# A graph attention layer: source maxima and shift spreads moved ahead of the last value tiles, two value tiles moved into the first steps

## The reference

```
for h in range(8):
    Wx = x @ Ws[h] + Wb[h]
    s = Wx[v_tgt] @ a_w[h, :d] + Wx[v_src] @ a_w[h, d:] + a_b[h]
    s = leaky_relu(s, 0.2)
    alpha = segment_softmax(s, v_tgt, n)     # minus the segment's maximum, exp, divided by the sum
    out[h] = segment_sum(alpha[:, None] * Wx[v_src], v_tgt, num_segments=n)
x = layernorm(x + stack(out, axis=1))
```

## Time and profile before

| | us |
|---|---|
| median of 3 runs | 2437.59 |
| lowest and highest | 2435.18, 2441.69 |
| the profiled execution's own time | 2438.18 |
| its span | 2436.4 |

### The profile page before, as it was taken

How to read it: one execution, slowest core, us unless ns; L and a number is a source line. 1 busy time by engine, 2 the same in 40 slices (tenths; PEclk the granted TensorE clock), 3 DMA queues, 4 the chain that set the end, 5 groups by cost and what they waited for, 6 DMA issues and landing times. The chain is left out here.

```text
span 2436.4 us, 38708 instructions
## 1 busy us (share of the span) xinstructions
PE 2099.4 (86%) x14446; PEld 1586.3 (65%) x14446; DVE 1608.4 (66%) x3166; ACT 1020.9 (42%) x1498; POOL 644.7 (26%) x472
## 2 busy tenths in 40 slices
PE   6888978998899998899998899998885996888784
PEld 5885537887777887677887777887672553333331
DVE  8995264778564877564778554877535045899964
ACT  1112225667344666344666344666320032144442
POOL 0000025100553100554100554100520000386763
PEclk9999989999999999999999999999997997998886
DMA  1011311889321889321889320879327000000001
GB/s 58 34 44 45 103 46 51 146 146 165 78 66 40 147 142 158 87 66 33 147 143 164 87 66 26 151 140 161 96 110 186 12 4 21 1 0 0 1 0 42
DMA packets 488150, 195.74 MB, mean 80 GB/s; under 512 B 441077, under 2 KB 457461, under 8 KB 487969
## 3 DMA queue, kind: packets, MB, share of 16 engines
q1 hardware_dynamic: 487969, 193.31, 38.0%
HBM read 62.94 MB, written 25.45 MB: 36 GB/s over the span
## 5 line engine op out<-in xcount | busy, mean ns | idle before, releaser
L667 PE MATMUL psum<-turned_probability_parts,values_high 125*128 125x125 bf16 x1600 | 281.5, 222 | 59.3 <-DVEq L1520 23.7
L856 DVE CUSTOM_DVE_ANT_0 probabilities<-psum,counts 125x1250 f32<-125x1250 f32 x160 | 233.5, 1459 | 130.0 <-PE psum L669 129.7
L1367 ACT ACTIVATE probabilities<-probabilities,row_peaks 125x1250 f32<-125x1250 f32 x160 | 214.5, 1341 | 181.2 <-DVE row_peaks L860 181.0
L669 PE MATMUL psum<-turned_probability_parts,values_low 125*128 125x125 bf16 x1600 | 280.8, 221 | 0.0
L668 PE MATMUL psum<-turned_probability_parts,values_high 125*128 125x125 bf16 x1600 | 280.5, 221 | 0.0
L1529 DVE SCALAR_TENSOR_TENSOR probability_parts<-probabilities,row_masses,probability_parts 125x1250 bf16<-125x1250 f32 x160 | 245.7, 1536 | 9.2 <-ACT probability_parts L1377 8.6
L1890 POOL TENSOR_TENSOR logs_and_shifts<-logs_by_source,target_shifts_spread 125x1250 f32<-125x1250 f32 x80 | 208.0, 2616 | 127.0 <-ACT target_shifts_spread L2023 67.9
L1377 ACT ACTIVATE probability_parts<-probabilities,row_masses 125x1250 bf16<-125x1250 f32 x160 | 214.0, 1338 | 40.3 <-DVE row_masses L868 34.0
L2129 PE MATMUL psum<-probabilities_turned,values_and_ones 125*65 125x512 f32 (+1 forms) x480 | 198.6, 560 | 21.8 <-ACT probabilities_turned L2040 11.4
L667 PEld LDWEIGHTS psum<-turned_probability_parts,values_high 125*128 125x128 bf16 x1600 | 159.0, 99 | 80.7 <-issue 79.0
L450 ACT ACTIVATE norm_std<-norm_moments,norm_eps 125x1 f32<-125x1 f32 x120 | 35.2, 294 | 365.8 <-DVE norm_moments L446 365.8
(11 more groups left out here) (292 smaller groups left out, 5123.0 us busy)
## 6 DMA issues: line engine op xcount, KB each, us to landing
weight_stage<-in_L_gnn_m_w SPq DMA_DIRECT2D x32, 256.0 KB, 2.7
block_inputs_kept<-nodes SPq DMA_DIRECT2D x8, 896.0 KB
counts_kept<-counts_by_target_rows SPq DMA_DIRECT2D x10, 625.0 KB, 3.5
counts_by_target<-counts_kept SPq DMA_DIRECT2D x1, 6103.5 KB
logs_kept<-counts SPq DMA_DIRECT2D x1, 5468.8 KB
nodes<-block_inputs_kept SPq DMA_DIRECT2D x12, 448.0 KB
turned_probability_parts<-probability_parts SPq DMA_TRANSPOSE x320, 3.6
logs_by_source<-logs_kept SPq DMA_DIRECT2D x1, 4375.0 KB
```

The costliest lines, as they stand in the source:

```text
L667: pe.matmul(out, lh, rh, start=first, stop=False, skip_group_check=True)
L669: return pe.matmul(out, ll, rh, start=False, stop=last, skip_group_check=True)
L856: dve.tensor_tensor_reduce(prob[0:TILE, T % 2, :], scores, fx.count_src[0:TILE, i, 0:NODES], scale, MASKED, ALU.add, ALU.max, p[:, 0:1]).t ...
L1367: nc.scalar.activation(prob[0:TILE, T % 2, :], prob[0:TILE, T % 2, :], ACT.Exp, bias=fx.peak[0:TILE, T % 2, 1:2], accum_out=fx.mass[0:TILE ...
```

## The change

The arithmetic is the same. The order and three places in memory change:

- All of head 0's peaks, its `shift_of`, its turning and its three spread pieces come ahead of value tiles 6 to 9 on TensorE. VectorE does ten peaks, then two value tiles, and so on, in place of six (or four) peaks and one.
- Value tiles 8 and 9 (`EARLY_VALUES` = 8) are made within steps 0 and 1, in bank 7: on TensorE behind the step's source spread and ahead of `weigh(0)`, on VectorE behind the peaks of steps 0 and 1.
- On TensorE the source spreads of cuts 1 and 2 of head 0 stand behind value tiles 2 and 4.
- Each probability and shift buffer is a tensor of its own (rounded up to 32 bytes). Shift buffer 0 and probability buffers 0 and 1 lie behind `nodes_turned`, shift buffer 1 and probability buffers 2 and 3 on it. ScalarE's wait for all value tiles is gone; TensorE waits for the first eight before `weigh(0)`, and for the tenth before it turns head 1's shift.

The diff, without the lines in which only an index changes form:

```diff
@@ -1826,8 +1826,12 @@
         x_t = packer(nc, TURNED_AT)("nodes_turned", [128, CHUNKS, NODES], F32)
-        prob = packer(nc, TURNED_AT)("probabilities_turned", [128, 4, NODES], F32)
-        shifts = packer(nc, TURNED_AT + PLANE)("target_shifts_spread", [128, 2, NODES], F32)
+        place = packer(nc, TURNED_AT + PLANE)
+        shifts = [place("target_shifts_spread_0", [128, NODES], F32)]
+        prob = [place(f"probabilities_turned_{k}", [128, NODES], F32) for k in range(2)]
+        place = packer(nc, TURNED_AT)
+        shifts.append(place("target_shifts_spread_1", [128, NODES], F32))
+        prob += [place(f"probabilities_turned_{k}", [128, NODES], F32) for k in range(2, 4)]
         offset = packer(nc, SLOT_A_AT + TILES * NODES * 4 + 16)("logs_and_shifts", [128, 2, NODES], F32)
@@ -1853,10 +1857,15 @@
+        def value_bank(t):
+
+            return t % 2 if t < EARLY_VALUES else 7
+
         def region(n):
...
         PIECES = ((0, 500), (500, 1000), (1000, NODES))
+        EARLY_VALUES = TILES - 2
         PEAKS = 3 * TILES
@@ -1962,16 +1971,25 @@
             dve.wait_ge(cols_ready, 3)
-            for t in range(TILES):
-                if t < HALF:
-                    for n in range(6 * t, 6 * t + 6):
-                        peaks(0, n)
-                    if t == HALF - 1:
-                        shift_of(0)
-                else:
-                    for n in range(4 * (t - HALF), 4 * (t - HALF) + 4):
-                        peaks(1, n)
+            for n in range(TILES):
+                peaks(0, n)
+            value(0)
+            value(1)
+            for n in range(TILES, 2 * TILES):
+                peaks(0, n)
+            value(2)
+            value(3)
+            for n in range(2 * TILES, PEAKS):
+                peaks(0, n)
+            shift_of(0)
+            value(4)
+            value(5)
+            for n in range(TILES):
+                peaks(1, n)
+            for t in range(6, EARLY_VALUES):
                 value(t)
+            for n in range(TILES, 2 * TILES):
+                peaks(1, n)
@@ -1990,6 +2008,8 @@
                         peaks(g, n)
+                if T < TILES - EARLY_VALUES:
+                    value(EARLY_VALUES + T)
             for k in range(2):
@@ -2033,11 +2053,10 @@
-            act.wait_ge(v_ready, TILES)
             for T in range(STEPS):
...
                 act.wait_ge(scored, T + 1)
-                nc.scalar.activation(prob[0:TILE, T % 4, :], prob[0:TILE, T % 4, :], ACT.Exp,
+                nc.scalar.activation(prob[T % 4][0:TILE, :], prob[T % 4][0:TILE, :], ACT.Exp,
                                      bias=column[0:TILE, j, HEADS3 + h:HEADS3 + h + 1], scale=1.0 / UNIT3).then_inc(exped, 1)
@@ -2068,10 +2087,14 @@
             def value(t):
-                if t >= 2:
+                if t == EARLY_VALUES:
+                    pe.wait_ge(piece_copied, 4)
+                elif t > EARLY_VALUES:
+                    pe.wait_ge(v_ready, t)
+                elif t >= 2:
                     pe.wait_ge(v_ready, t - 1)
                 for c in range(CHUNKS):
-                    mm = pe.matmul(bank(t % 2)[0:TILE], x_t[:, c, cols(t)], lw.w_sb[:, c, :], start=(c == 0),
+                    mm = pe.matmul(bank(value_bank(t))[0:TILE], x_t[:, c, cols(t)], lw.w_sb[:, c, :], start=(c == 0),
                                    stop=(c == CHUNKS - 1))
@@ -2094,7 +2117,7 @@
                 elif h == 1:
-                    pe.wait_ge(piece_copied, 4)
+                    pe.wait_ge(v_ready, TILES)
                 else:
@@ -2139,16 +2162,20 @@
             pe.wait_ge(bias_ready, 1)
-            for t in range(1, TILES):
-                if t in (2, 4, 5, 8):
-                    n = (2, 4, 5, 8).index(t) + 1
-                    spread_sources(n // 3, n % 3)
+            value(1)
+            value(2)
+            spread_sources(0, 1)
+            value(3)
+            value(4)
+            spread_sources(0, 2)
+            value(5)
+            spread_sources(1, 0)
+            shift_turned(0)
+            for k in range(3):
+                shift_piece(0, k)
+            for t in range(6, EARLY_VALUES):
                 value(t)
-                if t == 6:
-                    shift_turned(0)
-                if t in (7, 8, 9):
-                    shift_piece(0, t - 7)
-            pe.wait_ge(v_ready, TILES)
+            spread_sources(1, 1)
             pe.wait_ge(ones_set, 1)
@@ -2162,6 +2189,10 @@
                         shift_piece(h + 1, j - 5)
+                if T < TILES - EARLY_VALUES:
+                    value(EARLY_VALUES + T)
+                if T == 1:
+                    pe.wait_ge(v_ready, EARLY_VALUES)
                 if T >= 1:
```

More of the change, by code:

```diff
@@ L1889, in _ @@
                     pool.wait_ge(scored, T - 1)
-                nc.gpsimd.tensor_tensor(offset[0:TILE, T % 2, :], lw.logs[0:TILE, j, :], shifts[0:TILE, h % 2, :],
+                nc.gpsimd.tensor_tensor(offset[0:TILE, T % 2, :], lw.logs[0:TILE, j, :], shifts[h % 2][0:TILE, :],
                                         ALU.add).then_inc(offset_ready, 1)
@@ L1982, in _ @@
                     dve.wait_ge(pv, T - 3)
-                dve.scalar_tensor_tensor(prob[0:TILE, T % 4, :], region(3)[0:TILE], bend[0:TILE, j, h:h + 1],
+                dve.scalar_tensor_tensor(prob[T % 4][0:TILE, :], region(3)[0:TILE], bend[0:TILE, j, h:h + 1],
                                          offset[0:TILE, T % 2, :], ALU.max, ALU.add).then_inc(scored, 1)
@@ L2022, in shift_piece @@
                 act.wait_ge(piece, 4 * h + 2 + k)
-                nc.scalar.activation(shifts[0:TILE, h % 2, a:z], bank(7)[0:TILE, 0:z - a], ACT.Copy).then_inc(piece_copied, 1)
+                nc.scalar.activation(shifts[h % 2][0:TILE, a:z], bank(7)[0:TILE, 0:z - a], ACT.Copy).then_inc(piece_copied, 1)
             def copy_out(h):
@@ L2128, in weigh @@
                 for a, z in CUTS:
-                    mm = pe.matmul(region(0)[0:WIDTH, a:z], values[0:TILE, j, h, :], prob[0:TILE, T % 4, a:z],
+                    mm = pe.matmul(region(0)[0:WIDTH, a:z], values[0:TILE, j, h, :], prob[T % 4][0:TILE, a:z],
                                    start=(j == 0), stop=(j == TILES - 1))
```

2 lines of the change are left out of this document (1 added, 1 removed).

## The result

The changed kernel took 2452.34 us (median of 6 runs, 2446.76 to 2455.55) against 2440.30 (6 runs of the kernel before beside it, 2435.18 to 2441.96). The ratio is 1.0049, with a 95% interval of 1.0032 to 1.0066: 12.0 us slower, where 9 was forecast and the range reached to 2454. Measured once more, 12 runs against 29 of the kernel before, it gave 1.0029 (1.0014 to 1.0044), 7 us. The two together say slower by 0.3 to 0.5%, some 7 to 12 us.

A forecast was written before the change was run, and what follows sets the result against it. The chain through GpSimd's first sums to step 4's score, then mostly VectorE and TensorE, was taken as the bound. Step 4 7.7 later plus 1.3 for shift buffer 1 gave 9.0 on 2438.18: 2447 us, range 2440 to 2454.

The forecast's parts named there:

- The gain: Prologue, head 0's shift ahead of value tiles 6 to 9: GpSimd starts at 2098.4, not 2106.13, 7.7 us earlier.
- The source spreads behind value tiles: Prologue, cuts 1 and 2 of head 0: VectorE waits for spreads queued behind value tiles 2 and 4, 5.2 us each.
- Tiles 6 and 7: Prologue, TensorE behind the third shift piece: tile 6 lands at 2101.5, tile 7 at 2105.0, delaying head 1's peaks.
- Tiles 8 and 9 in the steps: Steps 0 and 1: VectorE waits for both tiles, tile 8 taking 5.27; step 4 comes 7.7 us later.
- Carried to the end: From step 4 to the end: VectorE's waits for TensorE pass wholly into the time, 7.7 us; chance 0.65.
- The rival by which a head's boundary makes it up: Head boundaries: lateness partly made up where TensorE ends the wait, part of half hidden; 2441 to 2444.9 us, chance 0.25.
- a sign of being wrong: Behind step 4: the prediction is wrong if the distance between the two kernels shrinks from there on.
- The third operation of `shift_of`: Heads 1, 3 and 5 at j = 4: shift buffer 1's address makes it 0.44 us longer, 1.3 us in all.
- half hidden: Rival: no measurable change, as the clock stays up or a head's boundary partly absorbs lateness; 2441 to 2444.9, chance 0.25.
- The copies beside GpSimd: Value tile copies 8 and 9 in steps 0 and 1: not slowed by GpSimd's sums, nothing added.

The follow-up runs named there:

- the repetition: The changed kernel, unaltered, measured and profiled once more against the kernel before: ratio 1.0029 (1.0014 to 1.0044).
- the run with the new places alone: The kernel before in its old order, with only the changed kernel's places of probability and shift buffers: ratio 0.9973 to the kernel before.
- the PSUM pair: Peak scores of `shift_of` kept in PSUM, in the changed kernel (0.9927) and in the kernel before (0.9884), both ratios to the unedited kernel before.
- the first profiled pair: First profiles of the changed kernel and the kernel before: spans 2445.0 and 2436.4 us; measured ratio 1.0049.

## Why the prediction held, and where its sizes were off

- *The gain is real and not reached.* Forecast: GpSimd 7.7 us sooner. Measured: 8.6 sooner, then idle for 12.45.
- *The source spreads behind value tiles.* Forecast: VectorE idle 5.2 and 5.2. Measured: 5.32 and 3.49, and 5.32 and 6.25 in the repetition. Moving them back recovered step 0 wholly and 5.1 us of step 4. The first tile ran at the lower clock, as taken; the second did so in one profile and not in the other, behind the same idle time.
- *Tiles 6 and 7.* I took 3.6 and 3.5 for them; they took 9.85 together. The clock was down here, behind the short waits among the shift pieces, and I had no term for it. This mis-sized term is 2.7 us (1.6 in the repetition).
- *Tiles 8 and 9 in the steps.* Forecast: waits of 3.3 and 1.4 us. Measured: 4.58 and 1.43, tile 8 taking 6.31 where 5.27 was taken. With the term before it, step 0 came 4.6 later and not 2.8, step 2 11.5 and not 8.5, step 4 10.9 and not 7.7.
- *Carried to the end.* Forecast: all of it. The repetition and the run with the new places alone show it most cleanly, 11.6 us at step 4 and 11.5 at the end; the PSUM pair has 7.7 at step 4 and 10 in the time, and in the first profiled pair step 4 to the end differs by 1.0. The rival by which a head's boundary makes it up fell. Against the kernel before, the repetition's distance does shrink behind step 4, from 11.5 to 8.5, which the prediction named as a sign of being wrong; it is still 14 at the shift of the seventh head, and goes down in that head, where the kernel before has its 17.1 us of low clock.
- *The third operation of `shift_of`.* Forecast: 0.42 to 0.44 longer in heads 1, 3 and 5, from the address of a shift buffer. The traces show just that. But its 1.3 us on the time is the step that failed: alone, the new places made the kernel some 6 us faster (0.9973), and moving shift buffer 1 back in the changed kernel did nothing that could be measured. Why the places make the old order faster is not shown; that the clock's course in the heads moves with them is the likely reason. That the sum came near is in part luck, since this error and those in the clock behind waits go opposite ways: the order of work alone, taken as the changed kernel's 1.0029 to 1.0049 against 0.9973, costs 0.56 to 0.76%, 14 to 19 us (11.6 at step 4), and not 7.7. And the measured 7 to 12 us lie on both sides of the 0.3% (7.3 us) below which the prediction put its *half hidden* rival.
- *The copies beside GpSimd* took 0.69 each, as costed.

## What to carry to other kernels

When instructions are regrouped on one engine, look at each in-order queue for what stands behind a wait that now comes later: here two small matmuls behind two value tiles cost 5 to 10 us, where the regrouping was to gain 7.7. A small operation on VectorE that reads two SBUF tensors beside a busy GpSimd can be the dearest of its loop; one operand in PSUM removed 28 us here. And a change of a few tenths of a microsecond in a repeated step can go with a change of the time that is larger and of either sign (0.9973 and 1.0018 for the same order, the shift buffers 8 bytes apart), so price it by several runs, not by its row. The same holds for a clock dip read from one profile.

## What the runs showed of the hardware

- GpSimd's addition of two 1250-element float32 rows took 2.40 or 2.84 to 2.85 us, and which of them followed an 8-byte shift in the address of one input. The one floor per element in the Trainium skill, GPSIMD Engine Reference (3.1 Elementwise), doesn't show this; the measurement decides.
- Two VectorE operations in a row with two small SBUF inputs each (in the second both are the same tensor) took as long as a GpSimd operation beside them: 0.7 us to the end of the running one and 2.32 or 2.74 to the end of the next. With one operand in PSUM the second took 176 ns, and a third of the kind, with GpSimd idle, 170. The Trainium skill, SBUF — State Buffer (Who interferes with whom), says the same of instructions with two SBUF inputs, and the runs agree.
- TensorE's granted clock stayed at 1.2 GHz for 13.7 us in which the engine was busy all of the time (changed kernel), and for 17.1 with 15.94 busy; in other heads, with the same work, it rose after 6.8:

```profile
2133.40:2147.10 13.70, 13.70 (x31) 6.35 (x30) 9.30 (x21) 5.08 (x5) 7.64 (x3) 0.50 0.01 2
2147.10:2170.90 23.80, 19.84 (x66) 8.40 (x64) 21.64 (x53) 10.78 (x9) 17.16 (x8) 1.00 0.00 0
2170.90:2177.70 6.80, 3.63 (x6) 1.16 (x7) 6.70 (x14) 0.27 (x1) 2.92 (x2) 0.50 0.00 1
```

- Behind the same idle time of 3.26 or 3.27 us, the same eight matmuls of the same kernel took 3.70 us in one execution and 6.46 in another.
- Filling a wait with useless matmuls made the real ones behind it faster, 3.70 us in place of 5.39 and 6.31, and the kernel by 4 to 9 us.
